# GpSimd scales the token tiles itself before each scatter, and makes five low halves of shared features between second-choice scatters (two adaLN/MoE layers, one core)

## What is computed

```
# layer 0, mixture (top 1 of 16 experts, F = 256)
logits = x @ w_router.T
mask = one_hot(argmax(logits))
scores = sigmoid(logits) * mask
masked_inputs = scores.T[:, :, None] * x[None, :, :]      # the scaled tokens
gate_up = masked_inputs @ gate_up_proj                    # per expert
expert_out = (up * silu(gate)) @ down_proj
out = silu(x @ w_gate.T) * (x @ w_up.T) @ w_down.T + expert_out.sum(axis=0)

# layer 1, mixture (top 2 of 8 experts, F = 512, capacity 1280)
y = combine(silu(x_e @ w1 + b1) @ w2 + b2)
shared = silu(x @ sw1 + sb1) @ sw2 + sb2
out = y + 0.1 * shared
```

## Time and profile before

| | |
|---|---|
| median of 3 runs | 534.1 us (534.03 to 534.33) |
| span of the profiled execution | 586.4 us |
| the profiled execution's own time | the page gives none beside the span |
| PE busy in that span | 469.7 us (80%) |
| DVE busy | 247.4 us (42%) |
| ACT busy | 245.0 us (42%) |
| POOL busy | 236.3 us (40%) |
| mean granted clock of PE | 0.901 |

### The profile page before, as it was taken

The page is one execution under the profiler, slowest core; times in us unless marked ns, Lnnn a source line. Parts: engine busy times, 40 slices in busy tenths (PEclk is TensorE's granted clock), DMA queues, the critical chain, the costliest instruction groups (busy, mean ns, idle before and its releaser), DMA issues.

```text
span 586.4 us, 9983 instructions
## 1 busy us (share of the span) xinstructions
PE 469.7 (80%) x3128; PEld 394.6 (67%) x3130; DVE 247.4 (42%) x724; ACT 245.0 (42%) x593; POOL 236.3 (40%) x256
## 2 busy tenths in 40 slices
PE   6889897277888898899986854379899999999900
PEld 4778654235777675577775744159899999999900
DVE  1345684054555554256466631042433332333227
ACT  2233484032555552456345401024355455555515
POOL 2000057710555454500543777700056555556520
PEclk8899999569999998999977796569999999999965
DMA  9998224320222222500100111110123433313049
GB/s 265 331 381 325 89 68 138 106 67 19 71 64 65 70 55 64 162 1 1 37 23 28 46 51 45 51 52 2 46 76 99 131 104 96 112 48 94 23 146 300
DMA packets 66131, 57.96 MB, mean 99 GB/s; under 512 B 9485, under 2 KB 53152, under 8 KB 66099
## 3 DMA queue, kind: packets, MB, share of 16 engines
q1 hardware_dynamic: 58402, 43.99, 25.1%
q0 software_dynamic: 7168, 12.51, 6.5%
q10 hardware_dynamic: 528, 1.05, 0.5%
HBM read 30.28 MB, written 29.47 MB: 102 GB/s over the span
## 4 chain that ended last, share of the span: by engine, by line
PE 65%; another core or an unknown queue 12%; DVE 8%; issue 8%; DMA 2%; ACT 2%; POOL 1%; SPq 1%; POOLq 0%; DVEq 0%; ACTq 0%
PE PS L1468 10%; PE PS L1154 8%; PE PS L1198 5%; PE PS L1426 4%; PE PS L1277 4%; PE PS L1390 3%; PE PS L1228 3%; PE PS L1456 3%; PE PS L1458 3%; PE PS L1457 3%; PE PS L1262 2%; PE PS L1264 2%; PE PS L1263 2%; PE PS L1215 1%
## 5 line engine op out<-in xcount | busy, mean ns | idle before, releaser
L585 POOL DMA_INDIRECT back<-grp_y,grp_i x80 | 79.5, 994 | 100.6 <-DVE grp_y L1111 78.6
L567 POOL DMA_INDIRECT rows<-disp,slot x64 | 64.5, 1007 | 74.1 <-DVE slot L955 54.8
L1468 PE MATMUL PS<-w2r,act 128*128 128x128 f32 x640 | 77.9, 275 | 0.0
L1468 PEld LDWEIGHTS PS<-w2r,act 128*128 128x128 f32 x640 | 74.8, 192 | 0.2
L546 POOL DMA_INDIRECT back<-act,blk_i x48 | 47.0, 980 | 62.0 <-DVE act L915 43.1
L735 ACT ACTIVATE act<-PS,b1r 128x256 f32<-128x256 f32 x160 | 63.7, 476 | 18.7 <-PE PS L1458 11.2
L535 POOL DMA_INDIRECT rows<-disp,slot x32 | 33.0, 1032 | 81.8 <-ACT disp L631 73.3
L1111 DVE TENSOR_TENSOR grp_y<-PS,b2r 128x256 f32<-128x256 f32 x40 | 17.0, 424 | 92.4 <-PE PS L1468 57.8
L1426 PE MATMUL PS<-sw,act 128*128 128x128 f32 x256 | 37.0, 308 | 19.6 <-DVE acc L1045 12.6
L1426 PEld LDWEIGHTS PS<-sw,act 128*128 128x128 f32 x256 | 35.6, 222 | 20.9 <-issue 19.8
L687 ACT ACTIVATE act<-PS,sb 128x512 f32<-128x512 f32 x32 | 21.0, 687 | 66.3 <-remote 30.9
(11 more groups left out here) (215 smaller groups left out, 983.0 us busy)
## 6 DMA issues: line engine op xcount, KB each, us to landing
rows<-zrow SPq DMA_DIRECT2D x32, 258.0 KB, 4.7
grp_x<-rows SPq DMA_DIRECT2D x40, 129.0 KB
back<-zrow SPq DMA_DIRECT2D x8, 512.0 KB, 6.3
c0w<-in_f_gate_up SPq DMA_DIRECT2D x8, 512.0 KB
back<-back SPq DMA_DIRECT2D x16, 256.0 KB, 4.5
blk_x<-rows SPq DMA_DIRECT2D x48, 64.5 KB
acc<-in_x SPq DMA_DIRECT2D x8, 256.0 KB, 5.0
y0g<-back SPq DMA_DIRECT2D x8, 256.0 KB, 3.6
```

Source lines behind the costliest of these rows:

```text
L567: gp.indirect_dma_start(rows1, bass.IndirectOffsetOnAxis(ap=slot[:, k, t:t + 1], axis=0), disp[:, t, :], None, bounds_check=E1 * CAP - 1, ...
L585: gp.indirect_dma_start(back1, bass.IndirectOffsetOnAxis(ap=grp_i[v % NX][:, u:u + 1], axis=0), grp_y[k][:, u, :], None, bounds_check=last ...
L1468: last = mm(PS[5 + k][:, u * P:(u + 1) * P], act[k][:, c, u * P:(u + 1) * P], w2r[e][:, c, :], start=c == 0, stop=c == C1 - 1)
```

## The change

Layer 0: ACT's 32 scalings are gone. POOL scales each tile itself (`tensor_scalar`, 128x128) right ahead of the tile's scatter, and waits for its own result before the scatter. Before the first it waits for the sigmoid (`sg0`) and for all of `disp` (`tok_done`).

Layer 1: for the groups 3 to 7 DVE makes only the high half and tells it on a new semaphore `s_hi`; POOL makes the low half (`tensor_tensor`, 128x512), ahead of the second-choice scatters 0, 4, 8, 12 and 16, once `s_hi` and PE's `s_gu` allow it. Groups 0 to 2 stay with DVE.

```
--- before.py
+++ after.py
@@ -318,6 +318,7 @@
         s_sp = sem("s_sp")
+        s_hi = sem("s_hi")
         s_gu = sem("s_gu")
@@ -527,11 +528,14 @@
             pool.wait_ge(zero0, 16 * (NBLKP // 4))
             pool.wait_ge(codes0, 1)
+            pool.wait_ge(sg0, 1)
+            pool.wait_ge(tok_done, NG)
             for t in range(NT):
                 if t % (NT // 2) == 0:
                     pool.wait_ge(slots0, t // (NT // 2) + 1)
-                if t % G == 0:
-                    pool.wait_ge(scaled, t + G)
+                gp.tensor_scalar(disp[:, t, 0:H], disp[:, t, 0:H], score[:, t:t + 1], None,
+                                 ALU.mult).then_inc(scaled, 1)
+                pool.wait_ge(scaled, t + 1)
                 gp.indirect_dma_start(rows0, bass.IndirectOffsetOnAxis(ap=slot[:, 0, t:t + 1], axis=0),
                                       disp[:, t, :], None, bounds_check=NBLKP * P - 1,
                                       oob_is_err=False).then_inc(sc0, 16)
@@ -564,6 +568,12 @@
                     if k == 1 and t == 0:
                         pool.wait_ge(slots1, NT // RT + 1)
+                    if k == 1 and t % G == 0 and t // G + 3 < NG:
+                        n = t // G + 3
+                        pool.wait_ge(s_hi, n - 2)
+                        pool.wait_ge(s_gu, C1 * (n - 1))
+                        gp.tensor_tensor(xl[n % 2][:, :], featT[:, n * GP:(n + 1) * GP],
+                                         xh[n % 2][:, :].bitcast(fp32), ALU.subtract).then_inc(s_sp, 1)
                     gp.indirect_dma_start(rows1, bass.IndirectOffsetOnAxis(ap=slot[:, k, t:t + 1], axis=0),
@@ -627,10 +637,6 @@
                     sc.activation(sil[:, c, :], PS[2 * c][:, :], ACT.Silu).then_inc(sil_done, 1)
-                for t in range(n * 2 * G, min((n + 1) * 2 * G, NT)):
-                    sc.activation(disp[:, t, 0:H], disp[:, t, 0:H], ACT.Copy,
-                                  scale=score[:, t:t + 1]).then_inc(scaled, 1)
-
                 for r in split_rounds(n):
@@ -987,6 +993,9 @@
                 f = featT[:, n * GP:(n + 1) * GP]
+                if n >= 3:
+                    v.tensor_copy(xh[n % 2][:, :], f).then_inc(s_hi, 1)
+                    return
                 link(v.tensor_copy(xh[n % 2][:, :], f))
                 v.tensor_tensor(xl[n % 2][:, :], f, xh[n % 2][:, :].bitcast(fp32), ALU.subtract).then_inc(s_sp, 1)
```

## The result

| | before | after |
|---|---|---|
| median of the timed runs | 534.2 us (534.03 to 534.43, 4 runs) | 580.4 us (579.77 to 580.95, 4 runs) |
| ratio after to before | | 1.087 (1.085 to 1.089) |
| profiled execution | 586.4 span | 578.0 span, 579.8 its own time |
| POOL busy | 236.3 us | 267.4 us |
| mean granted clock of PE | 0.901 | 0.900 |

The account below looks back on a forecast made before the run. The prediction took POOL's scatter chain to bound the timed kernel in both layers, with PE ahead. Layer 0's +29.5 and layer 1's +10.4 us gave 39.9 over 534.1, so 574 us, range 552 to 583.

Parts of the forecast that it names:

- The bound: Both layers' scatter stretches: timed kernel bound by POOL's chain, PE 7.7 us ahead in layer 0, 11.3 in layer 1.
- 5.03: End of the scatters, both layers: us from the last scatter's end until the first block's load has landed.
- the waits on 'remote' come with the recording: Scatter stretches of both layers: idle time on "remote" is only in the profiled run; 586.4 span against 534.1 median.
- The profiled span of 588 to 602: Whole changed kernel, profiled: layer 0 adds 15.6 us, layer 1 from 0 to -14.3, against the old span of 586.4.
- real covers: Profiled delay of first blocks beyond what scatters allow, 13.9 us in layer 0, 24.7 in layer 1, present in timed runs.
- rival (1): Both layers: "remote" waits are the kernel's own and hide added POOL time; +15.6 us (chance 0.06) or +1.3 (0.04).
- Layer 0, +29.5: POOL's scatter chain in layer 0: 31 steps each 0.94 us longer plus 0.37 at the start; 26.7 to 33.7 us.
- Layer 1, +10.4: POOL's second-choice scatters: first subtraction delays 3.0 us, four others cost 1.84 each; 9.2 to 12 us.
- The sum: Whole timed kernel: 29.5 + 10.4 = 39.9 us over 534.1, giving 574 us.
- (4): Layer 0: POOL's scalings wait out DVE's 16 two-input subtractions, 0.686 us each; +11.0, 585 us, chance 0.10.
- (3): Covers gone but POOL's 0.80 us wait for its own result hidden; +14.0 + 6.7, 554.8 us, chance 0.08.
- (2): Pauses cure the "remote" waits: no loss in layer 0, layer 1 blocks start earlier; -18, 516 us, chance 0.04.

Follow-up runs that it names:

- slots first: Kernel before, with DVE making layer 0's slots before its first-group products and POOL's code waits moved to the scatter needing them; 530.4 us, ratio 0.993.
- layer 0's part alone: Kernel before with only the scalings moved from ACT to POOL, layer 1 unchanged; 621.7 and 622.8 us, ratios 1.044 and 1.048, on 590 chips.
- layer 0's part and no collisions: Kernel before with POOL's scalings, and DVE's 16 two-input subtractions for gate-up low halves replaced by copies from PSUM; 568.1 us, one run, 534 chip.
- a tile ahead: Kernel before with POOL's scalings only, tile t + 1 scaled before tile t is scattered; 600.5 us, ratio 1.010, on a 590 chip.

## Why the prediction was right or wrong

**The bound: right, in layer 0 by estimate.** It said that the timed kernel hangs on POOL's scatters in both layers with PE ahead, and chose by the 52.3 us between span and median. The moves of the first blocks to 165 and 407, PE's 51.08 us on the load, and the absence of "remote" in every profile taken on a 534 chip (four kernels) bear it out for the changed kernel, and "slots first" for layer 1 of the kernel before (7.67 us on the load). For layer 0 of the kernel before no profile at 534 us exists. An estimate from "slots first" takes back the 3.7 us that its move cost PE (4.65 - 0.94) and has the sum ready at about 120.3; the scatters of the three profiles of the kernel before end at 120.06 to 122.42 and give the block 3.3 us later, at 123.4 to 125.8. PE is then ahead by 3 to 5 us, not by 7.7. The load lands 3.3 us (layer 0) and 3.9 us (layer 1) after the last scatter, not 5.03; the term stands on both sides and leaves the difference as it is.

**"The waits on 'remote' come with the recording": this step fell.** On 590 chips the timed runs are as long as the profiled one (median 596.0, the profiled 596.6), with the waits in it; on 534 chips recorded executions have none of the waits (median 580.4, the profiled 579.8 for the changed kernel; 530.4 and 530.4 for "slots first"). So the recording does not bring them, and what parts the two times is the chip or its condition at the time. One of the step's supports was misread as well: it put the waits on ACT, DVE and PE, and no wait of PE's in that profile is on "remote", only DVE's and ACT's. The profiled span of 588 to 602 that it gave for the changed kernel came out at 578.0, on a chip where no such wait stands in it. And the expert stages did have something to give: against "slots first" the old profile is 15.0 us later at the first block of layer 0, 5.7 longer in its 48 blocks, and 35.7 longer from the first scatter of layer 1 to its first block. That the rivals built on real covers came out low was right for the chip that the result was measured on; on a 590 chip rival (1)'s mechanism is the true one: with layer 0's part alone the first block moved by 23.3 us where the end of the scatters moved by 162.13 - 122.42 = 39.7, since the cover hid the rest. The Trainium skill's rule on the trace block (NOTIFIC — the notification-queue block, on overflow), which the step leaned on, is neither shown nor refuted here: nothing in these runs compares one chip with and without recording. Every execution of the groups, the 534 us ones too, has a span and a granted clock of its own on record, so none of them can be taken as surely free of it.

**Layer 0, +29.5: under-sized, about +38 to +42 measured.** With the same scatters as the earlier trace rows the chain of the kernel before ends at 120.06, and that of the changed one at 161.65: 41.6. The pattern was right to the hundredth in its gap (0.80). By terms:

| term | predicted | measured | for the stretch |
|---|---|---|---|
| scaling | 0.37, from the fills | 0.62 | +32 x 0.25 = 8.0 |
| collisions with DVE | 0 | 3.1 on scalings, 1.3 on a scatter | +4.4 |
| scatter | 0.98 | 1.02 | +31 x 0.04 = 1.2 |

29.5 + 8.0 + 4.4 + 1.2 = 43.1. The kernel before had late scatters of its own, 31 steps at 1.34 on average where an undisturbed one is 1.28, which is 1.9; 43.1 - 1.9 = 41.2. The term that was mis-sized is the scaling, by the choice of a `memset`'s 0.83 ns an element as the price of a scaling. The upper bound, 0.50 from the sums of two inputs at 2.0 ns, did not hold the 0.62 either: an element more costs 2.5 ns here.

**Layer 1, +10.4: over-sized, +4.4 to +6.5 measured.** The five steps were priced with the 0.80 of the earlier trace rows. That gap belongs to a scatter that waits for the instruction right ahead of it; the scatter behind a subtraction waits for nothing of it, and the row shows 0.17. So each costs 1.29 + 0.17 - 0.30 = 1.16 to 1.18, and five are 5.9. From the first block of layer 0 to that of layer 1 the changed kernel takes 242.0 and 240.2 us, the two kernels with POOL's scalings but DVE's low halves 235.8 and 235.5: 4.4 to 6.5. From its first second-choice scatter to the end of the last it takes 47.5 us (355.60 to 403.10) where the earlier trace rows have 42.2, not 10 more. The order of instructions shows no wait between the subtraction and the scatter; the prediction took the gap without asking what the scatter waited for.

**The sum** fell 6.3 us short because an error of about +10 and one of -5 met. It closes against the runs: the kernel with layer 0's part and no collisions is 33.7 us over the kernel before (568.1 against 534.4); the collisions add 4.5 and the low halves 4.4 to 6.5, together 42.6 to 44.7 of the 45.0 that the changed kernel took on that chip. (The 33.7 is one run, and less than 41.6 - 4.5 = 37. Up to 2.4 of the missing 3 us can be the kernel before itself, whose scatters end at 120.06, 120.31 and 122.42 in its three profiles and not always as early as in the earlier trace rows; the rest would be a first block that came later than its scatters allow, which no profile here shows. By time, layer 0 is 33.7 + 4.5 = 38.2, and this is the lower end of the +38 to +42.) That 574 came as near as 6 us to 580 is in part luck: two errors of opposite sign.

**The rivals.** (4), DVE and POOL holding each other up, is real at 4.5 us in layer 0, not 11: not every scaling meets a subtraction. It also goes the other way. DVE's two sums over `keep` in the changed kernel, the second beside POOL's subtraction at 367.10:

```profile
366.49 0.64 DVE L1086 TENSOR_TENSOR t<-keep,lg 128x256 f32<-128x256 f32 x1
367.17 1.65 DVE L1087 TENSOR_TENSOR t<-keep,lg 128x256 f32<-128x256 f32 x1
```

The second takes 0.60 in "slots first". It costs nothing, as DVE is off the path there. (3), the 0.80 hidden: refuted, but a distance of one scatter hides it (0.17 with a tile ahead). (2), faster, needed a step under 1.78 us in layer 0 and a real cover: neither on the 534 chips; on the 590 chips its layer-1 half came true, by 2 to 3%.

**Open.** What the "remote" waits are. They need a 590 chip, and there they stand beside long rows of scatters and, shorter, in the layer-1 blocks (41.0 us in 10 waits on `grp_y`); a step of 1.86 or 2.48 us, or a subtraction after every four scatters, takes them away in its own stretch. The loads of the profiles do not tell the two kinds of chip apart (`y0g<-back` lands in 3.4 us in the first repeat of the kernel before, in 3.3 in "slots first"). The whole change was never run on a 590 chip, nor either part of it in full alone on a 534 chip.

## What to carry to other kernels

Before work is given to an engine that is "1% of the chain", see whether its own row of instructions is what the next phase waits for: here 32 small scalings became 40 us because each stood between two links of such a row. If something must go between, keep a distance between the instruction and the one that waits for it: a tile ahead turned a gap of 0.80 us into 0.17. And when the profiled span and the timed median differ by more than a few us, the profile shows another condition than the time does; layer 1's part of this change is 2 to 3% faster in the one and, by estimate, 4 to 6 us slower in the other, so take both again on one chip before anything is concluded.

## What was not expected of the hardware

- One program, 534 us on one chip and 588 to 596 on two others, the kernel before at a mean granted clock of PE of about 0.935 there and 0.90 here, here with waits on DVE and ACT that the profile ties to nothing in the program, 86.5 us on DVE's lines 1043 and 1111 alone.
- POOL starts a scatter 0.30 us after another scatter, 0.17 after a compute instruction that it does not wait for (0.27 behind the change of codes in "slots first"), and 0.80 after one that it waits for.
- POOL's scaling of 128x128 by a column takes 0.62 us, 0.46 for 128x64.
- A scatter takes longer beside DVE's subtractions of two SBUF inputs: 1.25 to 1.47 us in place of 0.98 in the kernel before, and once 2.30 in place of 1.02, at the same place in both profiles of the changed kernel and in both of layer 0's part.
